# Attention values normalised by VectorE in their own PSUM bank and regrouped over DRAM, with value products in runs of four units

## The reference

```python
xn = _layernorm(x, axis=-1)
q, k, v = (split_heads(xn @ W.T + b) for W, b in ...)      # 4, 16, 1024, 16
q, k = rope(q), rope(k)
att = softmax(where(tril, q @ k.T / 4, -inf))
y = (att @ v), heads put side by side                      # 4, 1024, 256
attn = y @ Wo.T + bo
mask = the 4 largest of softmax(xn @ router_w.T + router_b) of each token
h = relu(where(mask, xn @ w1.T + b1, 0))                   # 1024 hidden units in 16 blocks
return x + attn + (h @ w2.T + b2)
```

## Time and profile before

| what | before |
|---|---|
| median of 3 runs | 864.9 us (863.66 to 865.03) |
| the profiled execution | 864.99 us, of which the span of its instructions is 863.2 us |
| granted TensorE clock | 0.998 |
| busy: TensorE, VectorE, ScalarE, GpSimd | 841.0, 537.9, 458.0, 281.5 us |

### The profile page before, as it was taken

The page is one execution under the profiler, slowest core; times in us unless marked ns, Lnnn a source line. Parts: engine busy times, 40 slices in busy tenths (PEclk is TensorE's granted clock), DMA queues, the critical chain, the costliest instruction groups (busy, mean ns, idle before and its releaser), DMA issues.

```text
span 863.2 us, 15180 instructions
## 1 busy us (share of the span) xinstructions
PE 841.0 (97%) x5458; PEld 506.2 (59%) x5458; DVE 537.9 (62%) x1729; ACT 458.0 (53%) x1068; POOL 281.5 (33%) x298
## 2 busy tenths in 40 slices
PE   5999999999999999999999999999999999999997
PEld 4676455545456555556656656555656656565664
DVE  6848967676876557465775756657566665656201
ACT  2523455665656555455564554646465554646553
POOL 3475237536440078061641028524420002010000
PEclk9999999999999999999999999999999999999999
DMA  8672314232503162231410235140250314000001
GB/s 274 240 207 98 75 47 138 90 75 75 147 3 76 31 190 76 75 75 65 116 45 6 70 99 147 41 110 1 76 148 2 75 55 121 2 2 1 3 1 49
DMA packets 45674, 69.65 MB, mean 81 GB/s; under 512 B 5152, under 2 KB 20384, under 8 KB 45600
## 3 DMA queue, kind: packets, MB, share of 16 engines
q1 hardware_dynamic: 45600, 68.69, 27.3%
HBM read 38.93 MB, written 29.75 MB: 80 GB/s over the span
## 4 chain that ended last, share of the span: by engine, by line
PE 90%; DVE 4%; DMA 2%; ACT 1%; SPq 1%; issue 1%; POOL 0%; DVEq 0%; ACTq 0%
PE o_bank L1047 16%; PE banks L1031 15%; PE banks L965 14%; PE banks L940 12%; PE banks L953 12%; PE banks L914 6%; PE banks L1018 3%; PE banks L1034 3%; PE banks L923 3%; PE banks L980 2%; PE banks L944 1%; DVE banks L1257 1%; DMA k_st<-term_scratch 1%; DVE part_max L1254 1%; PE banks L1004 1%; SPq L551 1%
## 5 line engine op out<-in xcount | busy, mean ns | idle before, releaser
L831 ACT ACTIVATE probs<-banks 128x512 f32<-128x512 f32 (+3 forms) x768 | 337.5, 498 | 259.0 <-PE banks L1034 175.5
L1031 PE MATMUL banks<-q_st,k_st 99*128 99x512 bf16 (+3 forms) x768 | 241.5, 327 | 1.8 <-DVE row_max L1257 1.1
L965 PE MATMUL banks<-k_st,q_st 96*128 96x512 bf16 (+3 forms) x768 | 237.6, 327 | 2.0 <-DVE part_max L1254 1.0
L1254 DVE TENSOR_REDUCE part_max<-banks 128x1 f32<-128x512 f32 x256 | 161.2, 682 | 51.9 <-PE banks L965 51.3
L1257 DVE CUSTOM_DVE_ANT_0 banks<-banks,tri,part_max 128x512 f32<-128x512 f32 (+3 forms) x256 | 132.0, 555 | 83.2 <-PE banks L965 77.0
L1257 DVE CUSTOM_DVE_ANT_0 banks<-banks,tri 128x512 f32<-128x512 f32 (+3 forms) x256 | 121.3, 513 | 69.6 <-PE banks L965 69.1
L682 POOL TENSOR_SCALAR max_neg<-row_max 128x16 f32<-128x16 f32 x32 | 8.1, 253 | 421.1 <-DVE row_max L1257 421.1
L1047 PE MATMUL o_bank<-probs,v_sb 128*17 128x512 f32 (+3 forms) x1536 | 143.2, 490 | 0.0
L940 PE MATMUL banks<-xnT,w_sb 128*128 128x256 f32 x512 | 135.4, 388 | 0.9 <-DVE row_max L1257 0.9
L965 PEld LDWEIGHTS banks<-k_st,q_st 96*128 96x128 bf16 x768 | 73.8, 98 | 88.0 <-issue 30.4
L953 PE MATMUL banks<-w_sb,hT 128*128 128x256 f32 x512 | 120.8, 382 | 0.0
(11 more groups left out here) (89 smaller groups left out, 762.2 us busy)
## 6 DMA issues: line engine op xcount, KB each, us to landing
term_scratch<-pieces SPq DMA_DIRECT2D x96, 256.0 KB
q_st<-term_scratch SPq DMA_DIRECT2D x16, 768.0 KB, 5.9
k_st<-term_scratch SPq DMA_DIRECT2D x16, 768.0 KB, 8.5
acc<-in_x SPq DMA_DIRECT2D x8, 512.0 KB, 4.0
out<-acc SPq DMA_DIRECT2D x7, 512.0 KB, 3.6
x_sb<-in_x SPq DMA_DIRECT2D x3, 1024.0 KB, 6.5
x_sb<-in_x SPq DMA_DIRECT2D x4, 256.0 KB, 3.7
w_sb<-in_w1T SPq DMA_DIRECT2D x1, 1024.0 KB, 9.4
```

The lines of the kernel that those rows point to most:

```text
L831: nc.scalar.activation(probs[:, u % P_SLOTS, h, 0:w], filled("score", n, k, h)[:, 0:w], ACT.Exp, scale=SCALE).then_inc(s_out, 1)
L965: nc.tensor.matmul(bank[:, 0:w], q_st[0:KROWS, at, h, i * P:(i + 1) * P], k_st[0:KROWS, at, h, c * HALF:c * HALF + w], start=True, stop=Tr ...
L1031: last = nc.tensor.matmul(bank[:, 0:w], k_st[0:SROWS, at, h, j * P:(j + 1) * P], q_st[0:SROWS, at, h, q0:q0 + w], start=True, stop=not dia ...
L1254: ins = nc.vector.tensor_reduce(part_max[:, h, at:at + 1], bank[:, 0:w], AX.X, ALU.max)
```

## The change

It takes the turns of the values off TensorE. VectorE turns `o_bank` in 32x32 blocks in place, so that each block has its queries on the partitions; it takes the reciprocals of the sums, multiplies them in, and turns the blocks back into `o_norm`. A DMA stores `o_norm` in DRAM, and another loads the 64 rows of each group, without the rows between the heads, into `yT`. The bias `bv` no longer goes into `yT`: it is multiplied with `Wo` once and added to `bo`. The last half of the last group skips DRAM: `wo_last` has the rows of `Wo` in the places of `o_norm`, and the rest of the product is done ahead of it. `pv` runs are of four units, and `probs` is a ring of 2304 columns for each head. `turn_maxima` becomes an ordinary matmul over 128 columns. `arrange()` now counts VectorE's other work as chores with costs, and puts a wide `max` between a narrow product and other work. At the start group 0's stacks are stored and loaded apart from those of group 1, and the first two tiles of `ffn` come after the first maxima.

```diff
-BANKS, P_SLOTS, STACKS = 7, 4, 3
+BANKS, P_COLS, STACKS = 7, 2304, 3
-RUN = 2
+RUNS = ((0, 1, 2, 3), (4, 5, 6, 7), (8, 9, 10, 11))
-         + values_of(0, *range(NT)) + proj(0, (2, 0), (2, 1), (3, 0), (3, 1)) + [("unselT", 0)]
-         + hid(0, 0, *range(FB)) + ffn(0, 0, 1))
+         + values_of(0, *range(NT)) + proj(0, (2, 0), (2, 1), (3, 0), (3, 1)) + [("bo",), ("unselT", 0)]
+         + hid(0, 0, *range(FB)))
+CHORE = {"norm": 4900, "turn": 2900, "route": 3000, "found": 6000, "stats": 800, "variance": 1800, "guess": 1000,
+         "newton": 1450}
...
+        if stop % NU in (0, 4):
+            chores.append((clock, scored + 8, ("norm", (stop - 1) // NU, 0 if stop % NU else 1)))
...
                 elif may_work and done + COST[works[0][0]] / 2 <= share - SPARE:
+                    if not wide and wide_max_ready():
+                        do_max()
                     done += do_work(works)
...
+            def store_y(n, c):
+                b = n // NG
+                if b >= 2 and n % NG == 0:
+                    sp.wait_ge(y_in[c], (b - 1) * Y_INC)
+                sp.wait_ge(normed, 2 * n + c + 1)
+                sp.dma_start(y_scratch[b % 2, n % NG, :, c * HALF:(c + 1) * HALF], o_norm[:, c, :]).then_inc(y_out[c], 16)
+            def load_y(b, c, first, stop):
+                sp.wait_ge(y_out[c], (b * NG + stop) * 16)
+                sp.wait_ge(low_done, chain(min(b + 1, B - 1), 2))
+                if b:
+                    sp.wait_ge(m_fill, M_COUNT["out", b - 1, 3])
+                at = first % 2 * GH * HD
+                values = y_scratch[b % 2, first:stop, :, c * HALF:(c + 1) * HALF]
+                values = values.rearrange("g (h v) q -> (g h) v q", h=GH)[:, 0:HD, :]
+                sp.dma_start(yT[at:at + (stop - first) * GH * HD, first // 2, c * HALF:(c + 1) * HALF],
+                             values).then_inc(y_in[c], 16)
...
                 place_maxima(n, 1)
                 load_stacks(n + 2)
+                if b:
+                    store_y(n - 1, 1)
+                    load_y(b - 1, 1, 2, 4)
+                store_y(n, 0)
                 place_maxima(n + 1, 0)
...
-                nc.scalar.activation(oT[:], o_bank[:], ACT.Copy).then_inc(o_out, 1)
...
-                nc.tensor.transpose(bank.bitcast(BF16)[0:NPIECE * GH * 4, 0:P],
-                                    max_pc[:, half].rearrange("p k r -> p (k r)"), identb[:]).then_inc(m_fill, 1)
+                nc.tensor.matmul(bank[:, 0:P], max_pc[:, half, :], identb[:], start=True, stop=True).then_inc(m_fill, 1)
-            def turn_o(n, c):
...
-                for t in range(4):
-                    last = nc.tensor.transpose(bank[:, t * P:(t + 1) * P], oT[:, t * P:(t + 1) * P], ident[:])
+            def biases():
+                pe.wait_ge(wo_in, 16)
+                pe.wait_ge(bv_spread, 1)
+                bank = free_bank("bo")
+                for k in range(KB):
+                    last = nc.tensor.matmul(bank[:, 0:D], bv_wide[:, k, :], wo_sb[:, k, :], start=(k == 0),
+                                            stop=(k == KB - 1))
...
+            def last_out_rest(t):
+                if t == NT // 2:
+                    pe.wait_ge(y_in[1], B * Y_INC)
+                bank = free_bank("outl", t)
+                tokens = slice(t * P, (t + 1) * P)
+                nc.tensor.matmul(bank[:, 0:D], yT[:, 0, tokens], wo_sb[:, 0, :], start=True, stop=False)
+                nc.tensor.matmul(bank[:, 0:D], yT[0:P // 2, 1, tokens], wo_sb[0:P // 2, 1, :], start=False, stop=False)
+            def last_out(t):
...
+                nc.tensor.matmul(banks[:, BANK["outl", t], 0:D], o_norm[:, 1, i * P:(i + 1) * P], wo_last[:], start=False,
+                                 stop=True).then_inc(m_fill, 1)
...
                 if j == 0 and (n or c):
-                    pe.wait_ge(o_out, 2 * n + c)
+                    pe.wait_ge(normed, 2 * n + c)
...
-                bank = filled("oT", n, c).rearrange("p (t h v) -> p t h v", t=4, h=GH)
-                link(nc.vector.reciprocal(recip[:, c], bank[:, :, :, HD]))
-                o = y_sb[:, 4 * c:4 * c + 4, g * GH * HD:(g + 1) * GH * HD].rearrange("p t (h d) -> p t h d", h=GH)
-                nc.vector.tensor_tensor(o, bank[:, :, :, 0:HD],
-                                        recip[:, c, :, :, None].broadcast_to([P, 4, GH, HD]),
-                                        ALU.mult).then_inc(m_out, 1)
+                dve.wait_ge(pv_done, n * NU + (NU if c else 4))
+                link(nc.vector.transpose(o_bank[:], o_bank[:]))
+                heads = o_bank[:].rearrange("p (q v) -> p q v", v=OW)
+                link(nc.vector.reciprocal(recip[:], heads[:, :, HD]))
+                link(nc.vector.tensor_tensor(heads[:, :, 0:HD], heads[:, :, 0:HD],
+                                             recip[:, :, None].broadcast_to([P, HALF // OW, HD]), ALU.mult))
+                if n:
+                    dve.wait_ge(y_out[c], n * 16)
+                nc.vector.transpose(o_norm[:, c, :], o_bank[:]).then_inc(normed, 1)
```

419 lines of the change are left out of this document (222 added, 197 removed).

## The result

The changed kernel takes 853.84 us (median of four runs, 853.02 to 854.43) against 864.4 of the kernel before; the ratio is 0.9878, with an interval from 0.9863 to 0.9894. It is faster by 10.6 us where 40 were forecast: 29.2 us above the predicted time, and above the range of 815 to 842.

The account below looks back on a forecast made before the run. TensorE's full stream was taken as the bound. Its parts sum to 39.4 us less, the end 1.5 and early stretch 2.5 less, new waits 3 more: 40.4 off the 863.2 us span, 822.8, so 824.6 us forecast; range 815 to 842.

Parts of the forecast that it names:

- Part 1: TensorE's stream: the turns of `oT` go, 31 fours at 0.43 us, 13.3 us less.
- part 2: TensorE's stream: 56 turns of `y_sb` at 0.11 us go, 6.0 us less.
- Part 3: Runs of `pv`: a fixed price of 0.22 us a run; 96 runs become 48, 10.6 us less.
- Part 4: Turns of the maxima: 128 columns instead of a narrow 48 save 0.19 us on each of 32, 6.1 us less.
- Part 5: Work behind narrow products on TensorE: 0.05 us at each of 86 places that go, 4.3 us less.
- Part 6: Added to TensorE's stream: the product of `bv` and `Wo`, two fp32 products of 256 columns, 0.9 us more.
- early stretch: From 54 to 110 us: `ffn` tiles behind first maxima let VectorE start earlier; 2.5 us less (4.5 less to 3 more).
- VectorE: Each normalisation takes 2.2 us instead of 0.7, 586 us busy in all; new waits 3 us, between nothing and 22.
- (b): Rival: VectorE comes late, each of 32 normalisations holds TensorE 0.25 to 0.75 us more; 832 to 849 us, chance 0.17.
- The end: From the last `pv` to the last addition: 6.6 us instead of 8.10, 1.5 less, with four 64-row products at 0.2 more.
- (c): Rival: the way over DRAM or SyncE's order is late, first scores wait 1 us a group; about 840 us, chance 0.04.
- (e): Rival: slower than before, long `pv` runs starved waiting for exponentials; 878 us at 1.2 us a run, chance 0.02.

Follow-up runs that it names:

- b8: b5 with one more 32x32-block turn on VectorE in each of the 31 normalisations, 22 us more VectorE work: 855.39 us, +15.6.
- b7: b5 with the turn of the maxima as an ordinary product with a stationary of 48 columns, not a transpose: 843.28 us, +3.5.
- f2: d1 with the last products over 128 rows and without the planner's rule for wide maxima: 833.87 us.
- e1: The changed kernel with VectorE's copy of `bv` moved behind the first rotations: 848.75 us, ratio 0.9811 to the kernel before.
- e2: The changed kernel with the copy of `bv` at its old place, as an instruction with two sources: 848.87 us, ratio 0.9816 to the kernel before.
- e3: The changed kernel with the first stacks' stores and loads back to the order and size of the kernel before: 847.44 us, ratio 0.9804.
- e4: The changed kernel with the edits of both e1 and e3: 841.8 us, ratio 0.9736 to the kernel before.
- b5: e4 with the two first `ffn` tiles put back ahead of the turns of the maxima: 839.77 us, ratio 0.9721 to the kernel before.
- c3: b5 with only the last of four operations per normalisation (values not divided by sums), and the planner's price at 1700 columns instead of 4900: 824.29 us, -15.5.
- d1: b5 with each normalisation planned and issued as two pieces, no operation left out: 834.9 us, -4.9.
- f1: d1 with the last products over 128 rows and both pieces of each normalisation two scores sooner: 830.91 us, ratio 0.9615 to the kernel before.

## Why the prediction was wrong

- **What bounds the kernel**: the reading held for the middle of the kernel before. It did not hold for what the change does: "as long as the others keep up" was the condition, and "it still has 240 us free" was taken as its proof. b8 shows that 22 us more of VectorE's work cost 15.6 with 28% of VectorE idle. The free time is not where the maxima wait.
- **Part 1 and part 2** right: the turns in the middle took 13.2 and 5.6 us, 0.118 and 0.117 each; 0.11 was forecast.
- **Part 3** right, and the inference in it too. In the middle the kernel before has 87 runs of two, the changed one 43 of four. From its start to the next product's a run takes its columns at 1.67 ns and 0.137 us more in the one, 0.147 in the other (medians), so the fixed part is the run's and not the unit's; and the 256 columns of bf16 ahead of a run take 0.20 us in both kernels where they take 0.11 ahead of other products. So 87 x (0.137 + 0.09) - 43 x (0.147 + 0.09) = 9.6 us went in the middle, for 9.7 forecast. What the prediction had not seen is that runs of two would also wait for the one bank, 14 to 29 us: long runs are worth more in this kernel than their fixed parts.
- **Part 4** right: 0.20 us a turn, and b7 shows that it is the width. The Trainium skill's rule that the prediction set against it (Perfetto Trace Analysis, "Transposes") did not decide the time: 48 columns wide the ordinary product costs the same 0.17 us as the transpose. No run has a transpose 128 columns wide.
- **Part 5** right in price and too large in sum. The first pass of `hid` or `ffn` takes 0.27 us behind a narrow product and 0.22 behind another, that of values 0.283 and 0.232, that of projections 0.483 and 0.432: 0.05 in each. But in the middle such places fall from 113 to 59, which is 2.8 us where 3.9 were forecast, and the rule for wide maxima, which brings 2.6 us there, takes back 1.6 at the start (f2).
- **Part 6** was 0.9 us of stream as forecast, but it brought the copy on VectorE with it, which the sum did not have. That is one failed step of the **early stretch**: 5 us (e1, e2), a copy of 0.3 us held by a memset.
- **Early stretch**, the other one: "the stack must be there 7 us earlier, for which half of the stores ahead of it are put behind" asked if the stack is late, and gave 3 us. The first maximum came 2.4 us late (56.36 against 53.92), but what stands behind the stores was later: GpSimd, 15.17 us, and the turn of the maxima, 10.80. The queue behind the moved step was not followed to its end. Undoing it brings 6.4 us (e3), with the copy moved too 12.0 (e4), and with the `ffn` tiles first 14.1 (b5). The move of the `ffn` tiles itself, which was to win 2.5 us, lost 2.0: in e4 TensorE stands 8.06 us at the first maximum with nothing in hand. Of the 18.7 us, b5 has 14.1 back at equal work, and c3 1.9 more, which are VectorE's burst. The other 2.7 are the gain of 2.5 that was in the sum and is in none of these kernels.
- **VectorE** was near in every duration (block turns 0.72 to 0.75 us for 0.687, 2.2 us in all, a total of 591.8 for 586) and wrong in its price: "I give new waits 3 us" was 15.5, of which 12.8 in the middle (b5 against c3). The bound of 22 held; the value taken was wrong because I looked for TensorE waiting on a late VectorE, rival (b), while the planner had turned this into another order, in which TensorE waits for ScalarE. The sign that was to show it, 10 us of TensorE's idle time released by VectorE, did not come either: from 110 to 834 us it is 0.6.
- **The end**: -0.7 instead of -1.5. The price of 64 rows was right per product (0.20), but there are eight changes and not four, since the way back to 128 rows costs as much: 0.8 us.

Sum of the failed terms: 18.7 us early, 9.7 in the middle and 0.8 at the end; they make up the 29.2. In the middle 12.8 us of cost stand against 3 forecast, and that is the miss; the other terms brought what was reckoned (c3's middle is 36.0 us shorter than before at equal work, the terms without the 3 us add up to 36.3). c3, which has the normalisation at the old price, measures 824.29 us, by chance the forecast: it is spared the 3 us of waits in the sum, and lacks the early 2.5 and 0.8 at the end.

None of the rivals named this. (b) had the engine, but not the size: 832 to 849 by itself. Neither (c) nor (e) came: from 110 us on only 0.2 us of TensorE's waits in the changed kernel are released by a DMA, and a run of four takes only its fixed part beyond its columns.

## What to carry to other kernels

Ask of a step that is moved what it holds until it is done, and follow the queue of every engine that waits for that, not only the transfer that was meant to be early. An engine's idle share is no room for longer bursts when it feeds the full engine through a few banks: add a burst on purpose, as b8 does, and measure its price before counting on the room. Where a planner sets the order, give it the new cost and compare what follows what in the old and the new order; and where work can be cut into pieces that let the feeding go on between them, cut it (d1 won 4.9 us so, and f1 2.1 more by issuing both pieces sooner). With the start put right and zero rows at the end as well, f1 is 33 us below the kernel before, against 10.6 for the change as it was.

## What the runs showed of the hardware that was not expected

- A copy in SBUF with one source, 256 columns of fp32, took 8.0 us beside a memset on GpSimd and ended with it; 0.29 us without it, and 0.43 us with two sources beside it. Shuffles and two-source operations of 512 columns ran beside the same memset at their usual 0.7 us.
- A contraction over 64 rows between contractions over 128 cost 0.20 us more at each change; zero rows were cheaper. A stationary side of 48 columns among ones of 128 cost the same 0.20 us, in an ordinary product as in a transpose.
- A block turn of 128x512 fp32, PSUM to PSUM or to SBUF, took 0.72 to 0.75 us, hardly more than an addition of that size (0.69).
- Twelve stores of 4 heads (128 KB each) ahead of the first stack's loads instead of twelve of 8 heads (256 KB) hardly shortened the way: 9.3 us from the end of the last low piece (41.31) to the load of the keys (50.57), against 10.4 in the kernel before (34.85 to 45.22).
